# Second expert loop's weights scaled by sums, split during the first expert loop, kept in DRAM and loaded per expert

## What is computed

```python
x = x + _L0_conv_ref(_ln_c(x), ...)          # means, maxima, gates, group norm
t = t + _L0_ffn_ref(_ln_t(t), ...)           # experts of width 512: w1, w3, w2
x = x + _L1_conv_ref(_ln_c(x), ...)          # 256x256 channel mix and bias
t = t + _L1_ffn_ref(_ln_t(t), ...)           # experts of width 1024: w1, w2, b1, b2

router = jax.nn.softmax(xf @ gate_w + gate_b, axis=-1)
k_scores, k_idx = jax.lax.top_k(router, K)
comb = jnp.zeros((t, e), x.dtype).at[jnp.arange(t)[:, None], k_idx].add(k_scores)
for i in range(e):
    h = jax.nn.silu(xf @ w1[i] + b1[i])
    y = h @ w2[i] + b2[i]
    out = out + y * comb[:, i:i + 1]
```

## Time and profile before

| | us |
|---|---|
| median of 3 runs | 1328.11 |
| runs | 1324.24 to 1330.5 |
| profiled execution | 1327.92 |
| its span, first to last instruction | 1326.2 |
| TensorE busy | 949.4 |
| VectorE busy | 882.8 |
| ScalarE busy | 525.5 |
| GpSimd busy | 438.9 |

### The profile page before, as it was taken

How to read it: one execution, slowest core, us unless ns; L and a number is a source line. 1 busy time by engine, 2 the same in 40 slices (tenths; PEclk the granted TensorE clock), 3 DMA queues, 4 the chain that set the end, 5 groups by cost and what they waited for, 6 DMA issues and landing times.

```text
span 1326.2 us, 25912 instructions
## 1 busy us (share of the span) xinstructions
PE 949.4 (72%) x7185; PEld 797.3 (60%) x7185; DVE 882.8 (67%) x1882; ACT 525.5 (40%) x1053; POOL 438.9 (33%) x486
## 2 busy tenths in 40 slices
PE   5210577546599999999500669458999999999943
PEld 4100456515488888888400549317888888888832
DVE  6999788897555555555499885774555555555545
ACT  5200223266454444444432534274433344433321
POOL 1285000000135555555423550003443344434310
PEclk8655795557799999999855975558999999999975
DMA  7000007805756556556586112004223322222257
GB/s 231 1 0 0 0 1 225 282 0 185 235 167 161 160 159 161 164 148 165 164 271 219 64 64 94 33 27 82 75 75 76 78 72 76 75 72 80 77 163 251
DMA packets 171935, 153.53 MB, mean 116 GB/s; under 512 B 89392, under 2 KB 147192, under 8 KB 171768
## 3 DMA queue, kind: packets, MB, share of 16 engines
q1 hardware_dynamic: 150920, 105.86, 28.2%
q0 software_dynamic: 14000, 38.82, 9.3%
q10 hardware_dynamic: 6976, 8.39, 1.9%
HBM read 102.68 MB, written 30.93 MB: 101 GB/s over the span
## 4 chain that ended last, share of the span: by engine, by line
PE 56%; DVE 19%; issue 9%; DMA 8%; ACT 3%; SPq 2%; DVEq 1%; POOL 0%; ACTq 0%; POOLq 0%
PE bank L719 25%; PE bank L740 19%; PE bank L654 4%; PE bank L571 3%; DMA xt<-region 2%; DVE tok L1410 2%; DMA wreg<-rows_y 2%; DVE region L1057 2%; DMA region<-rows_x,fetch_now 2%; PE bank L775 2%; ACT xt L880 2%; DVE xt L1069 2%; PE bank L626 1%; DVE region L1056 1%; DVE xn L1028 1%
## 5 line engine op out<-in xcount | busy, mean ns | idle before, releaser
L719 PE MATMUL bank<-xt,wreg 128*128 x3360 | 384.1, 275 | 28.4 <-DMA xt<-region 14.3
L719 PEld LDWEIGHTS bank<-xt,wreg 128*128 128x128 f16 x3360 | 327.3, 98 | 79.5 <-issue 38.2
L740 PE MATMUL bank<-wreg,region 128*128 128x256 f16 x2520 | 286.5, 273 | 0.0
L740 PEld LDWEIGHTS bank<-wreg,region 128*128 128x128 f16 x2520 | 246.6, 98 | 28.5
L914 ACT ACTIVATE region<-bank,b_t,fac 128x256 f32<-128x256 f32 x280 | 142.9, 561 | 226.9 <-PE bank L719 226.9
L502 POOL DMA_INDIRECT rows_y<-region,put_now x140 | 137.7, 983 | 237.3 <-DVE region L1393 140.8
L462 POOL DMA_INDIRECT region<-rows_x,fetch_now x144 | 142.6, 990 | 167.2 <-DMA xt<-region 89.5
L571 PE MATMUL bank<-ident,xn 128*128 128x128 f32 x256 | 56.5, 381 | 116.1 <-DVE xn L1028 108.7
L1378 DVE SCALAR_TENSOR_TENSOR region<-bank,fac,region 128x256 f32<-128x256 f32 x140 | 67.4, 483 | 88.4 <-ACT region L905 88.4
L1385 DVE TENSOR_SCALAR region<-region,fac 128x512 f16<-128x512 f32 x140 | 76.3, 545 | 69.5 <-ACT region L914 69.0
L571 PEld LDWEIGHTS bank<-ident,xn 128*128 128x128 f32 x256 | 45.6, 207 | 124.9 <-DVE xn L1028 115.0
(11 more groups left out here) (238 smaller groups left out, 1231.6 us busy)
## 6 DMA issues: line engine op xcount, KB each, us to landing
wreg<-in_L_ffn_w_dram SPq DMA_DIRECT2D x48, 512.0 KB, 6.0
region<-in_L_ffn_w_dram SPq DMA_DIRECT2D x72, 256.0 KB
wreg<-rows_y SPq DMA_DIRECT2D x48, 256.0 KB, 3.8
region<-in_L_ffn_w_dram SPq DMA_DIRECT2D x12, 1024.0 KB, 7.4
rows_x<-region SPq DMA_DIRECT2D x16, 512.0 KB, 3.1
wreg<-in_x_dram SPq DMA_DIRECT2D x4, 1024.0 KB, 9.7
wreg<-in_L_ffn_w_dram ACTq DMA_DIRECT2D x4, 1024.0 KB, 10.6
out_dram<-xt ACTq DMA_DIRECT2D x16, 256.0 KB, 3.4
```

The source lines that it names most:

```text
L719: last = pe.matmul(to, w[:, e, k, ws_, c * P:(c + 1) * P], x_cols[:, bass.ds(b, 1), :, xs_, k, :].rearrange("p j r n -> p (j r) n"), start ...
L740: last = pe.matmul(yb[:, r * C:(r + 1) * C], lhs[:, c, r * P:(r + 1) * P], w[:, e, c, ws_, :], start=first, stop=end, skip_group_check=True)
```

## The change

The scale of the second loop's weights is no longer taken from the maximum but from a sum. While VectorE works on the first convolution, SP loads 64 half pieces of 256 KB (`load_half`) into three buffers `sum_in`, each after the third last has been summed, and ScalarE sums absolute values over each row (`sum_pieces`: 20 between the two pairs of sigmoids, 44 behind them, and all before `deviation(4)`). `peaks1` and `scales(1)` move ahead of the first expert loop; GpSimd's reduction over partitions for them comes before that of the first loop's.

In each tile of `experts(0)` a piece of `v1` and one of `v2` are now split: ScalarE writes the high halves (`split_hi`, two instructions, ahead of its copy of the results), VectorE the low ones (`split_lo`, two, in the place of the one scan), and SP stores both to `split_v` in DRAM (`store_piece`, 512 KB). A tile's high halves wait until the store of the tile before has landed. Pieces are counted modulo 32; there are 35 tiles.

In `experts(1)` two experts' weights lie in SBUF (`v_s`). SP loads experts 0 and 1 behind the gathers and expert e + 2 when the last tile of expert e has ended (`load_v`, 4 transfers of 512 KB). The splitting between the loops is gone on all engines, with its loads and its waits.

The first loop's edges are read among the turns of its weights: one after each expert, on TensorE, ScalarE and VectorE. These loops over experts are now written out.

```diff
+            v1_rows, v2_rows = v1.rearrange("e (k p) f -> (e k) p f", p=P), v2.rearrange("e (q c p) d -> (e q) p c d", c=2, p=P)
...
+            for n in range(2 * PIECES):
+                free(sp, summed, n - 2)
+                load_half(sum_in[:, n % 3], n % 2, n // 2).then_inc(sum_loaded[n % 3], 16)
...
+            def store_piece(n):
+
+                sp.dma_start(split_v[bass.ds(n % PIECES // 4, 1), :, bass.ds(n % 4 * (2 * FH[1]), 2 * FH[1])].rearrange("a p n -> p (a n)"),
+                             piece_out[:, bass.ds(n % 2, 1)].rearrange("p j m s n -> p (j m s n)")).then_inc(piece_stored, 16)
+
+            def load_v(e):
+
+                for q in range(4):
+                    sp.dma_start(v_s[:, e % 2, q].rearrange("p m s n -> p (m s n)"),
+                                 split_v[e, :, q * 2 * FH[1]:(q + 1) * 2 * FH[1]]).then_inc(v_loaded[e % 2], 16)
...
                         if f == 0:
                             with sp.Fori(n, n + 1) as m:
                                 sp.wait_ge(piece_loaded, 32 * m + 32)
-                            with sp.Fori(n, n + 1) as m:
-                                sp.wait_ge(scanned, m)
                             load_piece(n + 1)
+                            split = sp.snap(n + 1)
+                            sp.wait_ge(piece_lo, split)
+                            store_piece(n)
+                    if f == 1 and e < E - 2:
+                        with sp.Fori(edges[e + 1], edges[e + 1] + 1) as m:
+                            sp.wait_ge(y_ready[1], m)
+                        load_v(e + 2)
...
-            for side in range(2):
-                load_outputs(0, side, side)
-            for h in range(1, 3):
-                for side in range(2):
-                    load_outputs(0, 2 * h + side, side)
-                load_stage1(h + 1, (h + 1) % 2)
-            load_outputs(0, HB - 2)
-            load_outputs(0, HB - 1, side=1)
-            reload_stage1(4)
-            for e in range(5, E):
-                reload_stage1(e)
+            for i in range(HB):
+                load_outputs(0, i, i % 2)
+            for e in range(2):
+                load_v(e)
...
+            def sum_pieces(first, end):
+                for n in range(first, end):
+                    act.wait_ge(sum_loaded[n % 3], 16 * (n // 3 + 1))
+                    act.activation(sum_in[:, n % 3], sum_in[:, n % 3], ACT.Abs, accum_out=sum_piece[:, n % 2, n // 2:n // 2 + 1]
+                                   ).then_inc(summed, 1)
+
             for r in range(2):
+                if r == 1:
+                    sum_pieces(0, 20)
                 for k in range(KC):
...
+            sum_pieces(20, 2 * PIECES)
             deviation(4)
...
+            def split_hi(n):
+
+                with act.Fori(n, n + 1) as m:
+                    act.wait_ge(piece_loaded, 32 * m + 32)
+                with act.Fori(n, n + 1) as m:
+                    act.wait_ge(piece_stored, 16 * m)
+                for m in range(2):
+                    act.activation(piece_out[:, bass.ds(n % 2, 1), m, 0].rearrange("p j n -> p (j n)"),
+                                   piece_in[:, bass.ds(n % 2, 1), m].rearrange("p j n -> p (j n)"), ACT.Copy,
+                                   scale=scl[1][:, bass.ds(n % PIECES // 4, 1), m:m + 1].rearrange("p a b -> p (a b)")
+                                   ).then_inc(piece_hi, 1)
...
             for e in range(E):
+                    if f == 1:
+                        pe.wait_ge(v_loaded[e % 2], 64 * (e // 2 + 1))
...
-                low1(e)
-            factors(1)
...
+            with dve.Fori(0, HB - 1) as i:
+                for j in range(2):
+                    norm(2, i + 1, j)
+                add_mixed(i)
             add_mixed(HB - 1)
-            dve.wait_ge(v1_lo, E)
```

More of the change, by code:

```diff
@@ L365, in turn_tiles @@
                 if f == 0:
+                    sp.wait_ge(w_turned, 6 * E)
                     load_piece(0)
@@ L760, in experts @@
                             down(f, e, n, h, halves)
+            edge = lambda e: pe.value_load(bounds[0:1, e:e + 1], min_val=0, max_val=TILES)
             routing(0)
-            for j in range(2):
-                stage_turns(0, j)
-            with pe.Fori(1, E // 2) as i:
-                for j in range(2):
-                    stage_turns(i, j)
-            experts(0)
+            edges = []
+            for e in range(E):
+                stage_turns(e // 2, e % 2)
+                edges.append(edge(e))
+            edges.append(edge(E))
+            experts(0, edges)
             def mix_channels(i, j):
@@ L792, in _ @@
             routing(1)
-            experts(1)
+            experts(1, [edge(e) for e in range(E + 1)])
             def turn_result(i):
@@ L949, in scale_v1 @@
-            def scale_v1(e):
-                stage = stage1_of(e)[:, 0]
-                act.activation(stage, stage, ACT.Copy, scale=scl[:, e, 0:1]).then_inc(v1_scaled, 1)
-            for e in range(E // 2):
-                high1(e, 0)
-                high1(e, 1)
-                scale_v1(e)
+            edge = lambda e: act.value_load(bounds[0:1, e:e + 1], min_val=0, max_val=TILES)
+            edges = []
+            for e in range(E):
+                for q in range(6):
+                    act.wait_ge(w_turned, 6 * e + q + 1)
+                    m, k = divmod(q, 2)
+                    to = (w1_s, w3_s)[m][:, e, k, 0, :] if m < 2 else w2_s[:, e, 2 * k:2 * k + 2, 0, :]
+                    src = zb[q][:] if m < 2 else turn[k][:].rearrange("p (c n) -> p c n", c=2)
+                    act.activation(to, src, ACT.Copy, scale=scl[0][:, e, m:m + 1]).then_inc(w_hi, 1)
+                edges.append(edge(e))
@@ L957, in _ @@
+            edges.append(edge(E))
+            experts(0, edges)
             deviation(2)
-            for i in range(HB):
-                e = E // 2 + i // 2
+            with act.Fori(0, HB) as i:
                 for j in range(2):
                     to_columns(2, i, j)
-                    if i % 2 == 0:
-                        high1(e, j)
-                    elif j == 0:
-                        scale_v1(e)
-            for by in (w_lo[1], v1_lo):
-                act.wait_ge(by, E)
@@ L1416, in combine @@
                                              ALU.mult, ALU.add).then_inc(y_used[q], 1)
+            peaks1()
             route(0)
             scales(0)
-            with dve.Fori(0, E // 2) as i:
-                for j in range(2):
-                    lows0(2 * i + j)
-            dve.wait_ge(w_lo[0], 6 * E)
-            factors(0)
-            experts(0)
-            scales(1)
+            scales(1)
+            edge = lambda e: dve.value_load(bounds[0:1, e:e + 1], min_val=0, max_val=TILES)
+            edges = []
+            for e in range(E):
+                lows0(e)
+                edges.append(edge(e))
+            edges.append(edge(E))
+            dve.wait_ge(w_lo, 6 * E)
+            for f in range(2):
+                factors(f)
+            experts(0, edges)
             def combine_tiles(i, side):
```

228 lines of the change are left out of this document (83 added, 145 removed).

## The result

The changed kernel takes 1358.75 us (median of 4 runs, 1357.27 to 1360.26) where the kernel before takes 1326.83 on the same chip: ratio 1.0234, 95% interval 1.0214 to 1.0254. It is 2.3% slower; 1291 was forecast. Its profiled execution took 1357.27 us, 29.35 more than that of before.

| stage | before | after | |
|---|---|---|---|
| start to the root of the first convolution (ScalarE's 128x64) | 136.73 | 146.77 | +10.0 |
| root to the first copy of results in the tile loop | 235.3 | 228.5 | -6.8 |
| first to last copy of results, 34 tiles | 277.5 | 346.5 | +69.0 |
| last copy to the gathers | 9.7 | 9.7 | 0 |
| gathers to the root ahead of the second convolution | 65.4 | 42.7 | -22.7 |

A forecast was written before the change was run, and what follows sets the result against it. VectorE bounded the first convolution and combination, TensorE the expert loops; the products' lines made 44% of the span. 1327.9 - 22.6 - 17.8 - 5.7 + 5.7 + 0.5 + 2 + 1 = 1291.0 us, range 1278 to 1318.

The forecast's parts named there:

- Combination, -22.6: Combination of the first loop's results: low halves, waits beside GpSimd's splits and small factor instructions leave VectorE's path, -22.6 us.
- that rival: Gathers bound the combination: at 180 GB/s 8 MB take 47 us, 11 us of gain stay out, 1302; chance 0.06.
- Second convolution, -17.8: Second convolution: four low halves go, 10.5 us, and the norms get faster by 7.3 us; together -17.8.
- Head, -5.7: Head of the first expert loop: TensorE's nine edge reads no longer stand between factors and first product, -5.7 us.
- Sums, +5.7: First convolution: ScalarE's sums of loaded pieces delay the root from 136.73 to 142.4 us, +5.7; bounds 0 and +23.7.
- p: Time per summed piece in the first convolution, from landing, sum and handovers over three buffers: taken as 1.2 us.
- The sentence on the drain: ScalarE's table switch before the root: a drain of 1.38 us beside the 1.28 load would make the sum 1.4 higher.
- Reductions of `peaks1`, +0.5: First convolution: the two reductions of `peaks1` add 0.5 us to VectorE's path.
- Tile loop, +2: First expert loop: the new splitting work fits within each tile and the store costs one hiccup, +2 us.
- The rival of the row supply: First expert loop: stores delay turns and fetches; mild 1313, worst 2.8 us a tile, 1384; chance 0.16, half mild.
- After the loop, +1: Behind the first expert loop: the last store follows the load by one issue and lands 3.1 us later, +1 us.
- second loop, 0: Second expert loop: loading the 2 MB of weights fits while the preceding expert runs, 0, up to +3 us.

The follow-up runs named there:

- the repaired kernel: Changed kernel with loads of pieces issued two tiles ahead into four slots and high halves waiting for store n-2, not n-1: 1304.86 us, ratio 0.9864.
- the small store: The repaired kernel with the store cut to 8 KB, and the second loop's loads too: 1295.46 us, ratio 0.976.

## Why the prediction was wrong, point by point

- **Combination, -22.6**: right. Gathers to root 65.4 and then 42.7, -22.7. The 32 first additions took 13.9 us, as the 13.8 forecast. No pair of additions (L1377) took more than 0.9 us, and the gathers came at 287 GB/s, so that rival was empty.
- **Second convolution, -17.8**: the total was right, from the first norm to the norms behind the last statistics 69.0 and then 51.6, -17.4; up to the second loop's first tile -19.0. That is partly luck. The 34 norms fell from 27.2 to 13.2 us, -14.0 and not -7.3, and the waits ahead of VectorE's additions, which the forecast left at 8.7, rose to 14.6, 6.4 of them for GpSimd. The main groups of the changed kernel, 772 to 828 us:

```profile
L1005 DVE TENSOR_SCALAR xn<-tok,mean,rstd 128x256 f32 x28 | 11.1, 455 | 0.9 <-PE bank L561 0.8
...
L1420 DVE TENSOR_TENSOR tok<-tok,bank 128x512 f32 x14 | 9.6, 684 | 13.5 <-PE bank L769 7.1 <-POOL tok L537 6.4
```

- **Head, -5.7**: right in size, factors to first copy -5.0, and -5.7 in the repaired kernel. The reason given was half of it: with TensorE's reads alone moved, ScalarE was held by its own loads and reads, and the time did not change.
- **Sums, +5.7**: the mechanism was right, the size not: +10.0. p was 1.24 us and not 1.2, which is 2.5 over 58 pieces. The rest lies at the heads of the two groups of sums, where three were put at 0.63 each: the fourth piece came 1.58 us late (at 69.76), and behind the second pair of sigmoids one piece and not three was ready. An accumulator read of 0.19 comes after each sum. The second pair of sigmoids ended at 91.4, 2.5 us late and not 1, and its first one began at 90.16 where it had 76.97 before; VectorE was ready for the root at the same time all the same. That the sums need not cost anything was not seen: ScalarE is busy for 5.32 of the 95 us in rows 2. The sentence on the drain from the Trainium skill, page "ScalarE: Activation LUTs", section "What ACT_TABLE_LOAD costs", isn't borne out here: the load starts 0.02 us behind the last accumulator read and the root 0.01 behind the load, so the switch cost 1.28.
- **Reductions of `peaks1`, +0.5**: can't be told. From the root to the factors are 218.4 us before, 216.7 in the changed kernel, and 214.4 in the run with TensorE's reads moved, whose code up to there makes the same.
- **Tile loop, +2**: this step failed, by 67 us. It read "the new work lies after the last high half ... ScalarE's copy of the results comes about 1 us later", which prices two instructions and neither of the two waits ahead of them. The rival of the row supply put the store's landing where it delays turns, and not where it delays ScalarE. Its worst case, 2.8 us a tile, was near the 2.0 measured, by another way, which is luck. "A load of the same size runs beside the fetches in each tile now, and TensorE has no gap" was no evidence: before, that load was waited for by VectorE's scan alone, the last thing in VectorE's tile, and at 559.39, in one such tile, it cost the scan 0.49 us and VectorE was still idle for 1.11 us behind it. The same transfer at the same place in SyncE's queue became critical because its reader moved ahead of the copy. Of the 69.0 us that the loop grew, 54.7 went with the two waits (the repaired kernel), 5.9 are the store's data, and 8.4 stay open.
- **After the loop, +1, second loop, 0**: 0 and -1.3. The first 0 holds because the last copy itself is late; in the repaired loop the stretch from it to the gathers is 13.9 us and not 9.7, and 10.4 with the small store, so 3.5 of it is the store's data.

How long the landing is matters less than who stands behind it; still, 4.6 us from issue to the reader's start is more than the 3.1 of the earlier trace rows. The Trainium skill, page "Perfetto Trace Analysis", section "DMA Instruction — HWDGE (DVE, Sync)", says that a transfer's semaphore moves only when its writes are confirmed, with "a surprisingly long delay especially when the write target is HBM". No run here shows such a delay: with the loads ahead only, a store of 512 KB lands 4.1 us after its issue, and the two loads that are issued in front of it, as many bytes, 4.2 us after the first's issue (medians).

## What to carry to other kernels

When a change gives an engine a new input, list for every wait what is queued behind it on that engine, and follow that list round until it comes back to the transfer waited for; if it does, the wait's full length is paid in each turn of the circle, whatever the busy times say. Two transfers queued at the same place hide each other: take both off before judging either. Then put filler work into the pauses that the timeline shows, no more of it than ends before the engine's next due instruction can start, and only where its own data is there by then.

## What the runs showed of the hardware

- An activation that sums (L833) is two instructions in the trace, 0.63 and 0.19 us, that overlap by 0.1.
- GpSimd's issue of a `put` takes 1.50 us where VectorE's low halves (two inputs in SBUF, L1298) run beside it, and 0.98 otherwise; the mean of the `put` is 1.23 us in the loop of the changed kernel (380 to 640 us) and 0.99 in the two runs with the high halves behind the copy. That the low halves are the cause is read from where the long ones stand, not tested.
- Two turns took 2.5 us to issue in an undisturbed tile and up to 3.95 in the repaired loop, at a DMA share of 0.74.
- In the changed loop TensorE is busy for 0.83 of the time, the others for about half and the DMA engines for 0.58, and it is 25% longer than the loop before.
